# Expert rows in one program part: scatters issued ahead of row fetches, two units turned early, last units reordered

## What is computed

```python
flat = h.reshape(-1, H)                        # 2048 x 512, normed
scores = jax.nn.softmax(flat @ router_w.T, axis=-1)
topk_w, topk_ids = lax.top_k(scores, K)        # 4 of 32 experts for a token
topk_w = topk_w / jnp.sum(topk_w, axis=-1, keepdims=True)
sort_idx = jnp.argsort(topk_ids.reshape(-1))
xs = jnp.take(flat, sort_idx // K, axis=0)     # rows, sorted by expert
gu = lax.ragged_dot(xs, w1, group_sizes)       # w1: 32 x 512 x 512
g, u = jnp.split(gu, 2, axis=-1)
ys = lax.ragged_dot(jax.nn.silu(g) * u, w2, group_sizes)   # w2: 32 x 256 x 512
y = jnp.zeros((T * K, H)).at[sort_idx].set(ys)
routed = jnp.sum(y.reshape(T, K, H) * topk_w[..., None], axis=1)
shared = jax.nn.silu(flat @ sg) * (flat @ su) @ sd
out = residual + (routed + shared).reshape(B, S, H)
```

## Time and profile before

| what | us |
|---|---|
| time, median of 3 runs (1616.9 to 1623.03) | 1617.81 |
| the profiled execution's own time | 1620.9 |
| its span | 1618.9 |
| PE busy | 1449.8 (90%) |
| DVE busy | 1308.3 (81%) |
| POOL busy | 1077.6 (67%) |
| ACT busy | 741.5 (46%) |

### The profile page before, as it was taken

One profiled execution on the slowest core, in us unless ns is written; L12 is line 12 of the kernel. 1 busy time (PEld: TensorE's weight loads), 2 busy tenths in 40 slices (PEclk: granted clock), 3 DMA queues, 4 the chain that ended last, 5 costly groups with the idle time before them and its releaser, 6 DMA issues. The chain is left out here.

```text
span 1618.9 us, 14732 instructions
## 1 busy us (share of the span) xinstructions
PE 1449.8 (90%) x4412; PEld 725.0 (45%) x4413; DVE 1308.3 (81%) x1931; ACT 741.5 (46%) x1160; POOL 1077.6 (67%) x545
## 2 busy tenths in 40 slices
PE   6578998889998889998798878899998999999996
PEld 3233443334443334443343323444445766667774
DVE  4599999999999999999999997355636777777772
ACT  4566665776656776657566664421000111111111
POOL 0199898999887999989999997230011455555453
PEclk9889999899999999999899999999999999999998
DMA  4540112410113411103310004021412888888895
GB/s 131 221 174 9 42 48 101 179 40 30 35 47 108 171 41 36 35 15 126 129 36 21 28 1 156 20 104 33 182 54 64 225 237 225 218 239 223 259 260 68
DMA packets 63823, 176.86 MB, mean 109 GB/s; under 512 B 10304, under 2 KB 15168, under 8 KB 55040
## 3 DMA queue, kind: packets, MB, share of 16 engines
q1 hardware_dynamic: 48128, 138.59, 24.8%
q0 software_dynamic: 15616, 37.32, 11.1%
HBM read 142.98 MB, written 32.85 MB: 109 GB/s over the span
## 5 line engine op out<-in xcount | busy, mean ns | idle before, releaser
L1342 POOL TENSOR_TENSOR h<-h,c_rep 128x2048 f32<-128x2048 f32 x128 | 579.3, 4530 | 31.2 <-DVE h L945 26.1
L1542 PE MATMUL bank<-h,ident 128*128 128x512 f32 x916 | 449.3, 634 | 93.0 <-POOL h L1342 74.2
L717 ACT ACTIVATE bank<-delta,a_neg 128x512 f32<-128x512 f32 x512 | 335.8, 682 | 178.9 <-DVE h L945 178.1
L1542 PEld LDWEIGHTS bank<-h,ident 128*128 128x128 f32 x916 | 180.6, 202 | 335.9 <-issue 210.9
L945 DVE TENSOR_TENSOR_SCAN h<-bank,state,h 128x512 f32<-128x512 f32 x256 | 306.0, 1260 | 0.5 <-ACT bank L717 0.5
L945 DVE TENSOR_TENSOR_SCAN h<-bank,h 128x512 f32<-128x512 f32 x256 | 290.7, 1199 | 2.8 <-ACT bank L717 2.6
L171 DVE STREAM_TRANSPOSE xT<-xg 32x256 f32<-32x256 f32 (+1 forms) x592 | 247.3, 418 | 56.0 <-DMA xg<-flat,slot_token 48.3
L935 DVE TENSOR_TENSOR h<-bank,b_rep 128x2048 f32<-128x2048 f32 (+1 forms) x105 | 227.5, 2184 | 35.7 <-ACT bank L708 24.2
L1703 POOL DMA_INDIRECT out<-y,slot_token x64 | 101.8, 1590 | 110.1 <-DMA out<-y,slot_token 65.2
L1329 POOL TENSOR_TENSOR h<-du,b_rep 128x2048 f32<-128x2048 f32 (+1 forms) x32 | 125.4, 3920 | 11.5 <-PE bank L1542 11.5
L1787 ACT ACTIVATE y<-y_ps,share 128x512 f32<-128x512 f32 x69 | 47.4, 687 | 185.3 <-PE y_ps L1935 152.3
(11 more groups left out here) (238 smaller groups left out, 1530.0 us busy)
## 6 DMA issues: line engine op xcount, KB each, us to landing
w_ring<-in_w SPq DMA_DIRECT2D x32, 1024.0 KB, 5.3
b_rep<-bcd SPq DMA_DIRECT2D x16, 1024.0 KB, 6.9
c_rep<-bcd SPq DMA_DIRECT2D x16, 1024.0 KB, 5.0
w_ring<-in_w SPq DMA_DIRECT2D x32, 512.0 KB, 7.4
w_in<-in_w_in_x SPq DMA_DIRECT2D x32, 256.0 KB, 2.6
w_res<-in_w_in_res SPq DMA_DIRECT2D x32, 256.0 KB, 2.6
xa<-in_x SPq DMA_DIRECT2D x20, 256.0 KB, 3.0
xb<-in_x SPq DMA_DIRECT2D x16, 256.0 KB, 3.0
```

Source lines behind the costliest of these rows:

```text
L717: eng.activation(da[j][:], delta[:, g % 2], ACT.Exp, scale=a_neg[:, col:col + 1])\
L1342: ins = eng.tensor_tensor(h[:, q], h[:, q], c_rep[:, Q * q:Q * q + Q, :], ALU.mult)
L1542: ins = eng.matmul(y_ps[:], c.ident[:], h[:, q, j, :], start=False, stop=(q == NQ - 1 and j == Q - 1))
```

## The change

1. *One part.* `experts` no longer opens a block. It returns one function for each engine, and the front calls each at the end of its own. The experts' PSUM tensors become banks that the front has (`g_ps`, `u_ps` and `y_ps` are all called `bank` in the listing of after). The barrier is gone; the waits that it covered are written out (`base_stored`, `upper_listed`, `gathered`). POOL goes on to fetch unit 2 right behind the first four slots.
2. *Two units turned in the closing.* DVE turns units 0 and 1 between the last mults and adds.
3. *POOL's order.* The scatters of a unit now stand ahead of the fetch that stood before them.
4. *The last units.* PE makes down(35) ahead of gate(36) and up(36), and ACT weights unit 35 ahead of silu(36).
5. *Weight loads.* The first load of a place waits for the last `up` that reads it (`up_done`), the second as before for `y_done`.

```diff
@@ front, scalar / vector / gpsimd / tensor / sync: each calls its part of experts
+                silu_experts(eng)
...
-                for u in range(1, UNITS):
+                for u in range(1, UNITS - 1):
...
-                c.turned(eng, 0, 2)
-                for i in range(UNITS - HC, UNITS):
-                    add(i)
+                c.turned(eng, 0, 2, 0, 10)
+                mult(UNITS - 1)
+                route(UNITS - 2)
+                c.turned(eng, 0, 2, 10, TURNS).then_inc(c.xT_ready, 1)
+                for v in (2, 3):
+                    eng.wait_ge(c.gathered[v], 16)
+                c.turned(eng, 1, 2, 0, 2)
+                add(UNITS - 4)
+                c.turned(eng, 1, 2, 2, 6)
+                add(UNITS - 3)
+                c.turned(eng, 1, 2, 6, 11)
+                add(UNITS - 2)
+                c.turned(eng, 1, 2, 11, TURNS).then_inc(c.xT_ready, 1)
+                add(UNITS - 1)
+                mult_experts(eng)
...
@@ experts, sync
-                    eng.wait_ge(S["y_done"], last_slot(place - RING) + 1)
+            eng.wait_ge(S["up_done"], unit_of(last_slot(place - RING)) + 1)
             eng.dma_start(c.w1r[:, u], dram.w1[ds].rearrange("a p k n -> (a p) k n")).then_inc(c.w_landed[u], 16)
+            eng.wait_ge(S["y_done"], last_slot(place - RING) + 1)
             eng.dma_start(c.w2r[:, u], dram.w2[ds].rearrange("a p k n -> (a p) k n")).then_inc(c.w_landed[u], 16)
...
@@ experts, gpsimd
+        eng.wait_ge(c.upper_listed, 32)
         for m in range(SHARED):
             first, b, u = m * SLOTS, m * RING, m * (RING + 1)
-                    gather(u + FED)
             scatter(first, b)
             scatter(first + 1, b)
-                    gather(u + FED + 1)
+            gather(u + FED)
             scatter(first + 2, b + 1)
             scatter(first + 3, b + 1)
-                    gather(u + FED + 2)
+            gather(u + FED + 1)
             scatter_piece(first + MIXED, 0, b + 1)
             scatter_piece(first + MIXED, 1, b + 2)
-                    gather(u + FED + 3)
+            gather(u + FED + 2)
             scatter(first + 5, b + 2)
             scatter(first + 6, b + 2)
             scatter_piece(first + MIXED, 2, b + 3)
-                    gather(u + FED + 4)
+            gather(u + FED + 3)
             scatter(first + 7, b + 3)
             scatter(first + 8, b + 3)
+            gather(u + FED + 4)
         for u in range(SHARED * (RING + 1), NU):
-                    gather(u + FED)
             for n in slots_of(u):
                 scatter(n, places(n)[0])
+            gather(u + FED)
...
@@ experts, tensor
-                for u in range(NU):
-                    if u + 1 < NU:
-                        gate(u + 1)
+        for u in range(NU - 2):
+            gate(u + 1)
             if single(u):
                 turn_act(u)
-                    if u + 1 < NU:
-                        up(u + 1)
+            up(u + 1)
             down(u)
+        down(NU - 2)
+        gate(NU - 1)
+        up(NU - 1)
+        down(NU - 1)
```

More of the change, by code:

```diff
@@ L163, in front, with turned @@
         c.xT = over("xT", "b_rep", [P, 2, KC, 2 * P])
-        def turned(eng, u, slots):
+        TURNS = (P // PIECE) ** 2
+        def turned(eng, u, slots, first=0, last=TURNS):
             x = c.xg[:, u % (AHEAD // 2), 0:slots, 0:DM].rearrange("p s (k m) -> p s k m", k=KC)
             out = c.xT[:, u % 2].rearrange("p k (s t) -> p s k t", s=2)
-            for rows in range(0, P, PIECE):
-                for cols in range(0, P, PIECE):
-                    ins = eng.transpose(out[cols:cols + PIECE, 0:slots, :, rows:rows + PIECE], x[rows:rows + PIECE, :, :, cols:cols + PIECE])
+            for n in range(first, last):
+                rows, cols = n // (P // PIECE) * PIECE, n % (P // PIECE) * PIECE
+                ins = eng.transpose(out[cols:cols + PIECE, 0:slots, :, rows:rows + PIECE], x[rows:rows + PIECE, :, :, cols:cols + PIECE])
             return ins
@@ L409, in front @@
         xa_at = {k: (n % 2, n // 2 + 1) for n, k in enumerate(xa_order)}
+        c.bank, c.upper_listed = bank, F["upper_listed"]
+        feed_experts, gather_experts, silu_experts, mult_experts, run_experts = experts(nc, c, dram, ctx)
         with nc.Block(no_gpsimd_drain=True) as block:
@@ L612, in _ @@
                 eng.wait_ge(F["upper_listed"], 32)
+                feed_experts(eng)
             @block.scalar
@@ L1409, in _ @@
                         .then_inc(c.gathered[n], 16)
+                gather_experts(eng)
             @block.tensor
@@ L1980, in build @@
         front(nc, c, dram)
-        experts(nc, c, dram)
 class Dram:
```

655 lines of the change are left out of this document (326 added, 329 removed).

## The result

The changed kernel takes 1664.1 us, the median of 4 runs (1662.1 to 1664.8), against 1619.96 of the kernel before in the same comparison: 1.027 times as long, with an interval of 1.0245 to 1.0296, or 44 us more. I had forecast 1639, with a range up to 1653.

What follows compares the result with a forecast made beforehand. PE was taken to bound the kernel, busy 240.67 of 245 us over most groups. Seam −6.4, groups +40.4, old waits −6.0, end −7.2 and weight loads 0 gave +20.8, on the 1617.8 median 1639 us, range 1604 to 1653.

Steps and rivals of the forecast that it cites:

- weight loads: 0: SP's weight loads: same bytes, each first load perhaps 3.4 us earlier, PE's waits name no weight load; no effect, 0.
- a load that collides with a fetch is in the 7.2 already: Weight loads: any delay to a colliding fetch was taken as covered by the assumed 7.2 us fetch landing.
- the forecast's own range: The range given to the forecast case itself, 1626 to 1648 us, with a chance of 0.46.
- The sum of the groups, +40.4: Five groups: fetches behind scatters make PE wait and gates run slow, 7.8 us a group plus 1.4 in the last; +40.4.
- the loss moves rather than goes: Groups: with the shortest piece, 6.52, u0+6 waits 0.1 but u0+7 waits 1.6 and u0+8 1.4; loss 7.1, not 7.8.
- The clock: 1.7 for each wait: PE's gates in the groups: behind waits of about 2 us a gate runs slow, 1.7 us each, ten times, 17 us.
- the two sums that I set side by side: Whole kernel: +20.8 with the clock's 17 us of slow gates, or +3.8 and 1622 us without.
- The seam: Joint of the two parts: barrier, waits for adds and second unit's turn, and slow gate go; −6.4, bounds −6.4 and 0.
- The end: From unit 34's first y: scatters, today 7.2 us late, would no longer be late; −7.2, bounds −7.2 and 0.
- Fast landings: Rival: fetches miss the weight loads and land in 3.5 us, pieces take 6.52; −17.6, 1600 us, chance 0.20.
- Late scatters: Rival: scatters stay late through the doubles, +5.0 on entry, and the end keeps its 7.2; +33, 1651 us, chance 0.18.

Runs made afterwards that it cites:

- fetch_first: The changed kernel with POOL issuing each row fetch ahead of the unit's scatters again, in groups and doubles; 1610.69 us, 0.995 of the kernel before.
- pieces_behind_fetches: The changed kernel with two of a group's five fetches (u0+6, u0+7) moved ahead of the single's scatter pieces; 1631.8 us, 1.0088 of the kernel before.
- old_loads: The changed kernel with both weight loads of a place waiting for the last down again, large one first; 1646.14 us, 1.0168 of the kernel before.
- clock_kept_half: The changed kernel with 36 unread matmuls added on PE, 3 to 7 ahead of each of eight waiting gates; 1651.05 us, 1.0197 of the kernel before.
- seam_alone: The changed kernel with POOL's order, weight loads and last units undone, leaving the joined part and two early turns; 1611.47 us, 0.995 of the kernel before.
- fetch_first_old_loads: The changed kernel with POOL's order and the weight loads both undone; 1609.41 us, 0.9939 of the kernel before.
- fifth_fetch_ahead: The changed kernel with fetches ahead of scatters again, and u0+8's fetch also ahead of the single's third piece; 1605.75 us, 0.992 of the kernel before.
- loads_back_to_back: The changed kernel with the next weight address read ahead of the waits, so a burst's two loads leave SP closer; 1651.45 us, 1.0201 of the kernel before.

## Why the prediction was wrong

**Right in direction and mechanism.** The loss is POOL's order: fetch_first takes 53 us back. Gates wait for turns, turns for fetches, fetches for pieces and scatters, and the clock falls behind each of the eight long waits. The time lies 11 us above the range, so the sizes were off, in two steps.

**The step "weight loads: 0" failed.** It counted bytes, asked whether PE waits for weights, and let the first load of a place go 3.4 us earlier. It did not follow SP's order: the large load now goes out, as a rule, right behind the small load of the place ahead, 16.0 us ahead of its own place's small one in the rows above (1261.77 to 1277.80) where it had been 0.52 ahead, and the reading of an address stands between the two that are now neighbours. The effect is 18 us (1664 to 1646), 13 of them by that gap, and none in the total when the fetches go first. The rows of the kernel before show no such gap; but the phrase "a load that collides with a fetch is in the 7.2 already" was the place to ask how much longer the collision lasts now. With this term right, the rest of the sum, 1646 against 1639, would have been inside the forecast's own range; in part that would have been luck, for the places of the waits were wrong there too.

**The sum of the groups, +40.4, stood for 62.** I had 23.4 of waits (five times 2.3 and 2.1, and 1.4) and 17.0 of clock. With old loads they are 32.9 and 14, 47 in all, so that 15 of the 22 missing go with the loads and the rest lies in the sizes. The pattern was wrong too. I had u0+4 and u0+6 wait in every group; in the trace it is u0+4 and u0+7 in the first, u0+6 in the second, and so on in turn (units 4, 7, 11, 14, 17, 21, 24, 27). The first group shows the terms. Unit 4's second fetch goes out 5.0 us behind the down (1244.30 to 1249.32) instead of 4.1 and lands in 7.7 instead of 7.2: it waits 3.80 instead of 2.3. Unit 6's second fetch lands in 3.7 and not in 7.2: it does not wait, and so unit 7 stood unprotected. Unit 7's chain is longer than I had put it down: unit 4's wait and slow matmuls ahead of it take 6.6 instead of 4.0, second scatter to third piece 8.95 (1278.85 to 1287.80) instead of 7.60, and its landing 8.03 instead of 7.2. The prediction's remark that the loss moves rather than goes was right; it should have made the waits larger and not kept them.

**The clock: 1.7 for each wait was too small.** I took one slow gate from the earlier trace rows; behind waits of 3.8 us and more the up is slow too, and a wait costs 1.5 to 2.9, 20 us in eight instead of 17.0 in ten. The Trainium skill, "TensorE: Matmul & The Clock Gate", section "HAM oscillation — how this bites in real kernels", says that a wait in every round makes each round begin at the low clock; the trace agrees, with 0.51 and 0.56 behind waits of the first and second group. Other runs show long waits that cost next to nothing, so the length of the wait alone does not set the price: in pieces_behind_fetches one of 3.88 us left the gate at 3.69 us (1310.34 above, granted clock 1.00 from 1310 to 1314), and in old_loads one of 1.98 made a gate and its up 8.83 instead of 7.07:

```profile
1490.85 8.83 PE L1912 MATMUL bank<-xT,w_ring 128*128 128x256 f32 x32 [1.98 <-issue]
```

And the two sums that I set side by side, with the clock and without, were not the full story: clock_kept_half takes 17 of the 20 us away and keeps 13 of them, and 4 are what PE would have waited anyway.

**The seam: right.** −6.4 forecast, −8.8 in the trace, of which 6.9 are the seam's, and 7 us in seam_alone.

**The end: right in the trace, but no gain of the whole change.** The chain from the first y of unit 34 to the end shrank by 7.8, and as I wrote, where fetches wait the scatters are in time. The order of the last units did not do it: fetch_first_old_loads has that order and is 7.4 us late. And where the fetches go first the moved loads have the same end (fetch_first, 0.3), in fifth_fetch_ahead without any wait paid for it. I had called it a gain of the change; here it was paid for in the groups.

**The rivals.** Fast landings (1600) did not come; the fetches' median landing was in fact shorter over the groups, 5.0 us against 6.4, and it did not help, since the late ones set the time:

```profile
xg<-flat,slot_token POOLq DMA_INDIRECT x38, 5.0
```

Late scatters (1651) came nearest to the time, but not in its way: the one long wait in the doubles (unit 27, 7.14 us) stands behind the fifth group's third piece, no later gate waited more than 0.35 us, and the end was not late.

## What to carry to other kernels

On an engine that issues in order, a prefetch must not stand behind work that waits for a result of the present step; put it ahead, even where the work behind it seems urgent. Where several chains are tight at once, do not add up the waits of one pass: one unit that waits shields the next, and one that does not exposes it, so cost the longest chain over two rounds. And a load that "only moves" is to be read in the listing of its queue, for what stands between two transfers now.

## What the hardware showed that I had not expected

A gap of 0.6 us between two loads of 0.5 and 1 MB made some 13 us of the whole (loads_back_to_back, 1651.45 against 1664.1, with intervals that just touch) where fetches stood behind scatters; with the fetches first the loads' whole move changed nothing in the total. Two waits of PE of like length can cost next to nothing or 2.8 us of slow matmuls (3.88 us at unit 8 of pieces_behind_fetches, 3.80 at unit 4 of the changed kernel). A matmul of 128x512 in f32 stands in the trace as two and took 0.9 us at full clock (7 in 6.28 us). Adding 32 us of idle matmuls to PE made the changed kernel 13 us faster (clock_kept_half).
